# A layer of decayed linear attention and a quantised feed-forward block: the input statistics of the next chunk moved up, and the output projection moved ahead of the quantisation

## The reference, cut to what matters

```python
def attention(x):                       # x: normalised
    q, k = l2norm(x @ Wq), l2norm(x @ Wk);  v = x @ Wv      # per head
    dt = softplus(x @ Wa + dt_bias)
    alpha = exp(-exp(A_log) * dt)
    cum_log = cumsum(log(alpha + 1e-8))
    l_mat = where(causal, exp(cum_log[:, None] - cum_log[None, :]), 0)
    out = (q @ k.T * l_mat) @ v
    out = out * rsqrt(mean(out * out) + 1e-6) * rms_w       # per head
    return out * silu(x @ Wg) @ Wo

def bitlinear(x, w, b):                 # 8-bit activations, ternary weights
    return activation_quant(rmsnorm(x)) @ weight_quant(w).T + b

xn = layernorm(x)
y = x + attention(xn) + bitlinear(gelu(bitlinear(xn, w1, b1)), w2, b2)
```

## Time and profile before

| | us |
|---|---|
| median of 2 runs | 6664.87 |
| the two runs | 6659.53, 6670.22 |
| the profiled execution | 6679.93 |
| its span on the slowest core (core 6) | 6678.4 |
| span of the fastest core (core 2) | 6638.9 |
| start of the first chunk's matmuls in phase B | 3948.3 |
| start of the last `PY * a2 + XRES` | 6674.0 |

### The profile page before, as it was taken

One profiled execution on the slowest core, in us unless ns is written; L12 is line 12 of the kernel. 1 busy time (PEld: TensorE's weight loads), 2 busy tenths in 40 slices (PEclk: granted clock), 3 DMA queues, 4 the chain that ended last, 5 costly groups with the idle time before them and its releaser, 6 DMA issues.

```text
span 6678.4 us, 54929 instructions; the slowest of 8 cores (6638.9 to 6678.4 us)
## 1 busy us (share of the span) xinstructions
PE 3194.4 (48%) x17994; PEld 1759.3 (26%) x17994; DVE 1866.1 (28%) x3514; ACT 1123.1 (17%) x1819; POOL 173.5 (3%) x310
## 2 busy tenths in 40 slices
PE   0255555454444555544434425555555555555555
PEld 0133333233333333333223301222222222222222
DVE  1233333333333333333333211211111122222222
ACT  0111111111111111111111111111111111111111
POOL 0000000000000000000000000000000000000000
PEclk9865655565656565555556556777777777777777
DMA  3110110110101011010011040000000000000000
GB/s 92 52 43 24 42 42 25 46 36 30 53 30 45 24 42 35 30 48 30 30 48 35 25 127 23 22 22 22 23 22 22 23 22 22 22 22 22 22 20 18
DMA packets 110215, 230.72 MB, mean 35 GB/s; under 512 B 54869, under 2 KB 55654, under 8 KB 104822
## 3 DMA queue, kind: packets, MB, share of 16 engines
q1 hardware_dynamic: 91702, 180.74, 9.0%
q0 software_dynamic: 18240, 46.46, 2.0%
HBM read 155.54 MB, written 58.72 MB: 32 GB/s over the span
## 4 chain that ended last, share of the span: by engine, by line
PE 44%; DVE 23%; issue 12%; DMA 7%; ACT 6%; SPq 6%; DVEq 1%; ACTq 0%; POOLq 0%
PE PY L1030 9%; PE PH L929 8%; PE PSM L715 5%; SPq L910 4%; PE PK L484 3%; ACT EBF L723 3%; DVE PBF L727 2%; DVE c_mxh L946 2%; PE PY L1046 2%; PE PVG L531 2%; PE PQS L503 2%; PE PSM L719 2%; PE PVG L518 2%; DMA WST<-w2t 2%; SPq L149 2%
## 5 line engine op out<-in xcount | busy, mean ns | idle before, releaser
L929 PE MATMUL PH<-W1Q,XQF 128*128 128x512 bf16 x2048 | 547.4, 415 | 575.5 <-DMA XQF<-scr_xq 478.4
L1030 PE MATMUL PY<-W2Q,HQF 128*128 128x512 bf16 x2048 | 577.3, 432 | 140.4 <-DVE HQF L1022 121.3
L940 ACT ACTIVATE HG<-PH,c_a 128x512 f32<-128x512 f32 x256 | 176.0, 687 | 2117.8 <-PE PH L934 2117.7
L731 PE MATMUL PVG<-VB,PBF 128*128 128x64 bf16 x512 | 108.3, 212 | 858.8 <-DVE PBF L727 858.8
L727 DVE TENSOR_TENSOR PBF<-PQS,EBF 128x128 bf16<-128x128 f32 x512 | 149.1, 291 | 1180.4 <-ACT EBF L723 1180.4
L723 ACT ACTIVATE EBF<-PSM,WNT 128x128 bf16<-128x128 f32 x512 | 187.6, 366 | 1589.0 <-PE PSM L719 1589.0
L484 PE MATMUL PK<-XNF,WK 128*128 128x128 bf16 x2048 | 186.1, 278 | 521.7 <-DVE XNF L476 521.7
L929 PEld LDWEIGHTS PH<-W1Q,XQF 128*128 128x128 bf16 x2048 | 191.7, 104 | 864.4 <-issue 718.6
L946 DVE TENSOR_REDUCE c_mxh<-HG 128x1 f32<-128x4096 f32 x32 | 141.4, 4420 | 979.8 <-ACT HG L940 979.8
L715 PE MATMUL PSM<-UFLAT,ONE 1*128 1x128 f32 x1024 | 405.4, 497 | 0.0
L1030 PEld LDWEIGHTS PY<-W2Q,HQF 128*128 128x128 bf16 x2048 | 200.2, 106 | 479.1 <-issue 346.6
(11 more groups left out here) (206 smaller groups left out, 4545.0 us busy)
## 6 DMA issues: line engine op xcount, KB each, us to landing
WST<-w1t SPq DMA_DIRECT2D x32, 1024.0 KB, 6.3
WST<-w2t SPq DMA_DIRECT2D x64, 512.0 KB, 4.2
XCH<-x SPq DMA_DIRECT2D x32, 512.0 KB, 7.9
XRES<-x SPq DMA_DIRECT2D x32, 512.0 KB, 6.3
y<-GT SPq DMA_DIRECT2D x32, 512.0 KB, 3.0
scr_xq<-XQB POOLq DMA_DIRECT2D x32, 256.0 KB, 2.3
scr_g<-GB POOLq DMA_DIRECT2D x32, 256.0 KB, 2.3
scr_att<-ATB POOLq DMA_DIRECT2D x32, 256.0 KB, 3.2
```

Of the source, the lines that this page charges most:

```text
L929: fns = [(lambda os=os, kt=kt, pp=pp: lambda e: e.matmul((PH1 if pp == 0 else PH2)[:, 0:512], XQF[:, kt * 128:(kt + 1) * 128], W1Q[:, kt * ...
L940: one("s", (lambda os=os, pp=pp: lambda e: e.activation(out=HG[:, os * 512:(os + 1) * 512], in_=(PH1 if pp == 0 else PH2)[:, 0:512], func= ...
L1030: lambda e: e.matmul(PY[:, ns * 512:(ns + 1) * 512], HQF[pp][:, i * 128:(i + 1) * 128], W2Q[:, kt * E + ns * 512: kt * E + (ns + 1) * 512] ...
```

## The change

Two edits.

In phase A, `phaseA_front(c + 1)` is called right behind the copy and store of the gate, ahead of the decay, and no longer between the two rounds of heads.

In phase B, gate, transposes and output projection are placed behind the eight Gelus and ahead of the maximum of `HG`. They go into a PSUM tile of their own, `PYW`, with the bias row first, and unscaled: the row operand is a constant row of ones, `ONESB`, and the gate is `(tanh + 1) * g` in one DVE operation. The reciprocal `ra2`, its DMA `RBROW`, the copy `RBROWB` and the scaling of the gate are gone. `PYW` is added to the result by one more DVE operation at the end. The tile `PB_TR` of the gate's transposes now shares its PSUM with `PB_TB1`.

```diff
         one("g", d_load(sG[c * C:(c + 1) * C, :], gb[:]),
             reads=[rgb], writes=[rb["scrG"]], inc=16)
+
+        phaseA_front(c + 1)
...
-            if r == 0:
-                phaseA_front(c + 1)
...
-    PB_TR = psB_("PB_TR", [128, 1024], BF16)
+    PYW = psB_("PYW", [128, 1024])
+    PB_TR = PB_TB1
+    rPTR = rPTB[0]
+    one("v", lambda e: e.memset(ONESB[:], 1.0), writes=[rb["ONESB"]])
...                                  (behind the eight Gelus:)
+        one("s", (lambda gbb=gbb: lambda e: e.activation(
+            out=GT[:], in_=gbb[:], func=AF.Tanh, scale=0.5))(),
+            reads=[rgbb, rb["GT"]], writes=[rb["GT"]])
+        one("v", (lambda gbb=gbb: lambda e: e.scalar_tensor_tensor(
+            out=GT2[:], in0=GT[:], scalar=1.0, in1=gbb[:],
+            op0=OP.add, op1=OP.mult))(),
+            reads=[rb["GT"], rgbb, rb["GT2"]], writes=[rb["GT2"]])
+        one("v", (lambda atb=atb: lambda e: e.tensor_mul(ATG[:], atb[:],
+                                                         GT2[:]))(),
+            reads=[ratb, rb["GT2"], rb["ATG"]], writes=[rb["ATG"]])
+        (eight transposes of ATG into PB_TR, copy to ATGF: as before)
+        fns = []
+        for ns in range(2):
+            fns.append((lambda ns=ns: lambda e: e.matmul(
+                PYW[:, ns * 512:(ns + 1) * 512], ONESB[:],
+                B2B[0:1, ns * 512:(ns + 1) * 512],
+                start=True, stop=False))())
+            for kt in range(8):
+                (matmul PYW <- ATGF, WO, 128x512: as before)
+        do("t", fns, reads=[rb["ATGF"], rb["WOw"], rb["ONESB"], rb["B2Bw"],
+                            rPYW], writes=[rPYW])
 
         one("v", lambda e: e.reduce_max(out=cl("mxh"), in_=HG[:], axis=AX,
                                         apply_absolute_value=True),
...
-        one("v", lambda e: e.reciprocal(out=cl("ra2"), in_=cl("a2")),
-            reads=[rc("a2")], writes=[rc("ra2")])
-        one("g", d_load(RBROW[:], COL["ra2"][:]), ...)
-        one("v", lambda e: e.tensor_copy(out=RBROWB[:], in_=RBROW[:]), ...)
-        (Tanh, scaling by ra2, two products, transposes, copy: all from here)
...
-        (bias row and output projection into PY: from behind the W2 loop)
...
             reads=[rPY, rc("a2"), rxres, ryout], writes=[ryout])
+        one("v", (lambda yout=yout: lambda e: e.tensor_add(
+            yout[:], yout[:], PYW[:]))(),
+            reads=[rPYW, ryout], writes=[ryout])
         one("y", d_load(dy[c * C:(c + 1) * C, :], yout[:]),
```

More of the change, by code:

```diff
@@ L880, in build_program @@
     PY = psB_("PY", [128, 1024])
-    PB_TR = psB_("PB_TR", [128, 1024], BF16)
+    PYW = psB_("PYW", [128, 1024])
     PB_TB1 = psB_("PB_TB1", [128, 1024], BF16)
     PB_TB2 = psB_("PB_TB2", [128, 1024], BF16)
+    PB_TR = PB_TB1
     rPH = [R(), R()]
-    rPY, rPTR, rPTB = R(), R(), [R(), R()]
+    rPY, rPYW, rPTB = R(), R(), [R(), R()]
+    rPTR = rPTB[0]
+    ONESB = sbB("ONESB", [1, 128], BF16)
+    rb["ONESB"] = R()
+    one("v", lambda e: e.memset(ONESB[:], 1.0), writes=[rb["ONESB"]])
     do("y", [(lambda i=i: d_load(W1Q[:, i * FF:(i + 1) * FF],
@@ L944, in phaseB_chunk @@
                 reads=[rPH[pp], rc("a1"), rb["HG"]], writes=[rb["HG"]])
+        one("s", (lambda gbb=gbb: lambda e: e.activation(
[8 more added lines that the diff above has]
+            reads=[ratb, rb["GT2"], rb["ATG"]], writes=[rb["ATG"]])
+        do("t", [(lambda i=i: lambda e: e.transpose(
+            PB_TR[:, i * 128:(i + 1) * 128], ATG[:, i * 128:(i + 1) * 128],
+            IDB[:]))() for i in range(8)],
+            reads=[rb["ATG"], cst, rPTR], writes=[rPTR])
+        one("v", lambda e: e.tensor_copy(out=ATGF[:], in_=PB_TR[:]),
+            reads=[rPTR, rb["ATGF"]], writes=[rb["ATGF"]])
+        fns = []
[5 more added lines that the diff above has]
+            for kt in range(8):
+                fns.append((lambda ns=ns, kt=kt: lambda e: e.matmul(
+                    PYW[:, ns * 512:(ns + 1) * 512],
+                    ATGF[:, kt * 128:(kt + 1) * 128],
+                    WO[:, kt * E + ns * 512: kt * E + (ns + 1) * 512],
+                    start=False, stop=(kt == 7)))())
+        do("t", fns, reads=[rb["ATGF"], rb["WOw"], rb["ONESB"], rb["B2Bw"],
+                            rPYW], writes=[rPYW])
         one("v", lambda e: e.reduce_max(out=cl("mxh"), in_=HG[:], axis=AX,
@@ L1035, in phaseB_chunk @@
                                     start=(q4 == 0 and i == 0),
-                                    stop=False))())
+                                    stop=(q4 == 3 and i == 7)))())
                 do("t", fns, reads=[rHf, rb["W2Qw"], rPY], writes=[rPY])
[L1038 to L1051, removed]
         one("v", (lambda yout=yout, xres=xres:
```

## The result

| | before | after |
|---|---|---|
| median of the runs, us | 6667.1 (42 runs) | 6690.7 (43 runs) |
| profiled execution, us | 6679.9 | 6678.0 |
| its span on the slowest core | 6678.4 | 6676.5 |

The ratio is 1.0032, 95% interval 1.0024 to 1.0041: the change makes the kernel 24 us slower, well outside its measurement's error though only a third of one per cent. The forecast was 6706 us and 0.6% slower. The two profiled executions are equally long by chance: single executions of the kernel before took 6658.0 to 6704.3 us. In some executions the cores of one die run at a lower granted clock than the others and the program takes some per cent longer; such executions are left out of every time, ratio and 95% interval here, and the ratios are worked out over all the others, so that they need not be the quotient of the two medians.

A forecast was written before the change was run, and what follows sets the result against it. Bound by chains of steps handing over between engines, no engine being near the span. Phase A +131 and phase B −90 us gave +41 on the 6664.9 us median: 6706 us, 0.6% slower; 8-in-10 range 6630 to 6755.

The forecast's parts named there:

- The front's price and refund: Phase A, 31 chunks: front exposed ahead of the decay, 10.86 us paid, 6.62 back between head rounds, +131 us.
- In-order issue: Phase A, DVE: L557 and all the decay wait until the front listed ahead is through, full 10.86 us exposed.
- The projection: Phase B's end: bias and projection leave the chain, −4.5 us a chunk, hidden in PE's idle stretch before the second product.
- Gate ahead of the maximum: Phase B, last Gelu to rounding: maximum 5.2 us late, rounding unmoved, 0 us a chunk, bounds −0.4 and +0.4.
- The table load: Phase B, ACT: second load now ahead of each chunk's first Gelu, +0.3 us a chunk, bounds 0 and 0.4.
- The sum: Phase B, added DVE operation between final operation and store: fully exposed, +1.4 us a chunk, bounds 1.2 and 1.5.
- the sum of 41 us: Whole kernel: phase A +131 and phase B −90 us together, +41 us, from +8 to +71.

The follow-up runs named there:

- the projection alone: The kernel before with only the change's projection, gate and sum edits, the front left between the rounds of heads: 6531.6 us, ratio 0.980.
- the early sum: The changed kernel with PYW added to the residual tile XRES behind a2, no sum behind the final operation: 6649.6 us, ratio to the kernel before 0.997.
- the spread front: The kernel before with projection, gate and sum edits, the front in ten pieces, one behind each of the first ten heads' products: 6299.2 us, ratio 0.944.

## Why the prediction was right

**The front's price and refund.** Predicted 10.86 us paid and 6.62 back, 4.24 a chunk, +131 us with a bound of +141. Measured 10.94 and 6.70, so 4.24. Phase A as a whole came out at +137 (core 6) to +152 us (core 2), on core 2 above the bound. What the sum left out is small and sits beside the front: the decay's next steps take 0.28 us longer (the bound named 0.3), the second round 0.17 and the projections 0.26. For the first of these the trace shows the cause: the decay's first two matmuls take 366 ns each in the mean, where they took 267 before. PE has now been idle for 12.8 us ahead of them and not 1.94, and the granted clock over them is 0.50 (2126 to 2128 us, core 6), where it was still 0.77 over them before (2058 to 2059). For the other two it shows none that was tested, and the 0.26 doesn't repeat: on core 6 the projections became 0.14 us longer, and in the two kernels with the front where it was (the one before and the projection alone, cores 2 and 6) they take 19.55 to 20.07. The last chunk, which had run without a front all along, was the best row of the profile: it gave the refund to 0.1 us.

**In-order issue, the step that decided the sign of phase A.** That all of the front stands ahead of `L557` was argued from the list's order. The experiment with the front ahead of the gate copy shows it: one place up the list hides 4.2 us more and takes 130 us off.

**The projection.** Predicted −4.5, measured −4.45 us. Hidden in its new place, as said, with 3.3 us to spare in the chunk shown; the low clock that it runs at costs nothing.

**Gate ahead of the maximum.** Predicted 5.2 us late at the maximum and the rounding where it was; measured 4.9 late and, from the last Gelu to the rounding, 0.4 us sooner (16.27 to 15.86 in the mean). This is the worst-sized term of phase B: at 0 it left 14 us out, at its bound of −0.4 it would have been right. Some 0.3 of it is the gate itself, whose first long operation takes 1.22 us with a bf16 result, not 1.28, and whose steps follow one another more closely than assumed. The rest is the chunk that was read: there the rounding came 16.00 us behind the maximum, and 16.17 in the mean of the 32. From maximum to rounding the sum of the prediction, 10.8 us, was met (10.84). The gate on ACT and DVE is a cost of 5 us that was predicted as a delay but not named as the change's main loss; the experiment with the gate inside the first product priced it at 163 us.

**The table load.** Predicted +0.3 us. PE waited for a Gelu twice in all the 32 chunks of core 6, 0.3 us together, and the first product became 0.12 us longer on core 2 and 0.03 on core 6: 6 us too much or more. ACT has 32 table loads at the first Gelu and none at Tanh; in the chunk shown Tanh at 4577.69 follows the Gelu at 4577.11 with no load between them. The table of the Trainium skill (ScalarE: Activation LUTs, Table sets: the hidden batching unit) names Tanh in the exp and sigmoid sets and not in the gelu set. Read as complete it asks for a second load there, and the trace doesn't bear that out.

**The sum.** Predicted +1.4, measured +1.53 in the mean of core 2, 1.34 in that of core 6, 1.45 in the chunk shown, exposed in full as the early sum shows.

**What lies beyond the steps.** The second product became 0.30 us shorter, 10 us in all, which was not forecast. Its first block isn't the reason: it starts at the low clock in both kernels and became 0.09 us longer. The later blocks are. Each takes 3.9 us, but one of them 5.2 to 5.5 us in 9 of the 32 chunks before (core 2) and in 2 after, 7 × 1.55 = 11 us. In one such block of the kernel before, from 4230.22 us on core 2, the granted clock fell with PE at work:

```profile
4232.00:4233.00 1.00, 1.00 (x3) 0.15 (x1) 0.00 (x0) 0.00 (x0) 0.00 (x0) 0.50 0.00 0
```

What makes it fall there, and why less often after the change, stays open.

Phase B thus gave 113 us on core 2 instead of 90, phase A cost 152 instead of 131. The two misses, of about 20 us each, cancel: that the sum of 41 us is so near to core 2's 39 is luck, and core 6, with 137 and 120, comes to 17. The measured 24 us lies between the two cores. The signs and causes of both halves were right; their sizes were each off by more than the sum shows.

## What to carry to other kernels

Work that is moved to "where the engine is idle" is hidden only by the idle time behind its own place in that engine's list: look at the idle time between the instruction in front of which it is put and its predecessor, and cut the work into pieces no longer than that. When a chunk repeats a chain 32 times, look first for the chunk in which a part is absent, since it prices the part better than any sum. And before the order within a stage is tuned, ask what the wait at its end is for: here 15 us a chunk were SP's order of a store and the next chunk's loads, more than all that the change moved.

## What the runs showed of the hardware

More work made PE faster: with the projection computed twice, 576 matmuls more, phase B became 99 us shorter (core 2). The granted clock stayed at its upper level over what had been an idle stretch of a few microseconds, and the block behind it took 3.99 us in the mean instead of 6.38.

Gelu and Tanh follow each other without a table load. Where Tanh follows the square root, in the kernel before, the change costs the load of 1283 ns and little else: the load starts 17 ns behind the square root's end, and Tanh 11 ns behind the load (median of 32).

In the head loop two lengths of the same handover occur. ACT's exponential starts either 0.38 or 0.50 us behind the start of the mask matmul that it waits for, and DVE's product either 0.47 or 0.54 us behind the exponential. By the medians of the 32 chunks, in the first round of the kernel before the first two heads have the short ones and the others the long ones; with pieces of the front between the heads, the fifth to eighth have the short ones too. These four make up the 0.75 us by which that round is shorter (19.17 to 18.42 us from the first to the last product, core 2), though ACT and DVE had more to do. How long the waiting engine had been idle doesn't decide it. Two heads of the kernel before, then one of the spread front:

```profile
1996.53 0.29 PE L719 MATMUL PSM<-MSKN,IDB 128*128 128x128 bf16 x1
1996.91 0.37 ACT L723 ACTIVATE EBF<-PSM,WNT 128x128 bf16<-128x128 f32 x1 [5.84 <-PE PSM L719]
...
2001.83 0.29 PE L719 MATMUL PSM<-MSKN,IDB 128*128 128x128 bf16 x1
2002.32 0.37 ACT L723 ACTIVATE EBF<-PSM,WNT 128x128 bf16<-128x128 f32 x1 [2.43 <-PE PSM L719]
...
1956.63 0.29 PE L733 MATMUL PSM<-MSKN,IDB 128*128 128x128 bf16 x1
1957.02 0.37 ACT L737 ACTIVATE EBF<-PSM,WNT 128x128 bf16<-128x128 f32 x1 [1.22 <-PE PSM L733]
```

The short one occurs with ACT idle for 5.84 and for 1.22 us, the long one for 2.43. What decides it was not tested.
